# A gated cross-attention layer: VectorE makes both rope products of a block in one instruction, and the maxima of a pair of items in one

## What is computed

```python
q_hk  = (layernorm(x) @ Wq.T).reshape(B, S, H, K)            # 16 heads of 128
q_big = einsum('bshk,hkq->bshq', q_hk, w_kc_q)               # 192 per head
q_big = q_big * cos + rotate_half(q_big) * sin               # rope over halves of 96
q_r   = einsum('bshq,hqr->bhsr', q_big, W_qr)                # 64
k_r   = einsum('bld,hdr->bhlr', rope(ctx), W_kr)
attn  = softmax(einsum('bhsr,bhlr->bhsl', q_r, k_r))         # 256 x 256
ctx_c = einsum('bhsl,bld->bhsd', attn, rope(ctx))
x     = x + tanh(g0) * (ctx_c through w_kc_kv and Wo)
x     = x + tanh(g1) * top-8-of-64 expert biases of layernorm(x)
```

## Time and profile before

| what | before |
|---|---|
| three timed executions | 262.70, 262.97, 262.98, median 262.97 |
| profiled execution | span 261.0 from first to last instruction; its time as a whole is not listed, the timed ones lie 1.7 to 2.0 above this span |
| TensorE matmul busy | 248.7 (95%) |
| VectorE busy | 180.5 (69%), 435 instructions |
| ScalarE busy | 144.0 (55%) |
| GpSimd busy | 136.6 (52%) |

### The profile page before, as it was taken

One profiled execution on the slowest core, in us unless ns is written; L12 is line 12 of the kernel. 1 busy time (PEld: TensorE's weight loads), 2 busy tenths in 40 slices (PEclk: granted clock), 3 DMA queues, 4 the chain that ended last, 5 costly groups with the idle time before them and its releaser, 6 DMA issues.

```text
span 261.0 us, 5668 instructions
## 1 busy us (share of the span) xinstructions
PE 248.7 (95%) x1961; PEld 187.1 (72%) x1961; DVE 180.5 (69%) x435; ACT 144.0 (55%) x440; POOL 136.6 (52%) x221
## 2 busy tenths in 40 slices
PE   6998999999999999999999999999999999889993
PEld 6874777587776878587857876787668758666871
DVE  3799889468775858386847774777658556676575
ACT  2720566574466454746445636656655477758551
POOL 3535139642782278525744565458624952527542
PEclk9999999999999999999999999999999999999997
DMA  6986542534100250124200300030003000000112
GB/s 229 231 224 162 178 102 82 136 106 136 41 0 3 50 173 3 43 58 92 82 3 0 80 4 0 14 70 3 1 0 82 2 3 0 1 3 0 41 34 91
DMA packets 17852, 16.72 MB, mean 64 GB/s; under 512 B 5152, under 2 KB 16544, under 8 KB 17824
## 3 DMA queue, kind: packets, MB, share of 16 engines
q1 hardware_dynamic: 17184, 15.64, 22.7%
q10 hardware_dynamic: 640, 0.72, 0.9%
HBM read 11.11 MB, written 1.05 MB: 47 GB/s over the span
## 4 chain that ended last, share of the span: by engine, by line
PE 79%; DVE 6%; POOL 5%; DMA 4%; ACT 3%; issue 3%; ACTq 0%; DVEq 0%; POOLq 0%
PE ring L1124 23%; PE probs_t L1308 12%; PE scores L1297 9%; PE context L1341 9%; PE ring L1165 5%; PE ring L1090 4%; PE ring L1188 2%; PE ring L1184 2%; PE ring L1186 2%; PE ring L1151 2%; DMA w_kc_q_sb<-in_w_kc_q 2%; POOL roped L599 2%; DMA moved<-cross 2%; PE ring L1113 1%; ACT probs L775 1%
## 5 line engine op out<-in xcount | busy, mean ns | idle before, releaser
L669 POOL TENSOR_SCALAR probs<-probs,inv_sum 128x256 f32<-128x256 f32 x128 | 59.6, 478 | 87.6 <-DVE inv_sum L1028 87.5
L785 ACT COPY probs_t_sb<-probs_t 128x512 f32<-128x512 f32 x64 | 37.6, 588 | 57.7 <-PE probs_t L1308 57.7
L775 ACT ACTIVATE probs<-scores,neg_max 128x256 f32<-128x256 f32 x128 | 59.9, 478 | 4.0 <-DVE neg_max L1022 3.8
L599 POOL TENSOR_TENSOR roped<-roped,cross 128x512 f32<-128x512 f32 x30 | 37.8, 1281 | 11.5 <-DVE cross L866 11.4
L1022 DVE TENSOR_REDUCE neg_max<-scores 128x2 f32<-128x512 f32 x64 | 40.9, 680 | 2.2 <-PE scores L1297 1.9
L1124 PE MATMUL ring<-xn_hi,a_hi 128*128 128x512 f32 x96 | 40.7, 424 | 0.1
L1308 PE MATMUL probs_t<-ident,probs 128*128 128x128 f32 x256 | 40.4, 280 | 0.3 <-POOL probs L669 0.3
L1124 PE MATMUL ring<-xn_hi,a_lo 128*128 128x512 f32 x96 | 37.7, 393 | 0.0
L865 DVE TENSOR_TENSOR roped<-ring,rope_q_sb 128x512 f32<-128x512 f32 x48 | 32.8, 684 | 6.9 <-PE ring L1124 6.7
L1124 PE MATMUL ring<-xn_lo,a_hi 128*128 128x512 f32 x96 | 37.5, 391 | 0.0
L1308 PEld LDWEIGHTS probs_t<-ident,probs 128*128 128x128 f32 x256 | 28.7, 140 | 9.8 <-issue 2.2
(11 more groups left out here) (116 smaller groups left out, 464.3 us busy)
## 6 DMA issues: line engine op xcount, KB each, us to landing
moved<-cross SPq DMA_DIRECT2D x30, 128.0 KB, 2.3
wo_t_sb<-in_wo_t SPq DMA_DIRECT2D x4, 512.0 KB, 4.8
w_qr_sb<-in_w_qr SPq DMA_DIRECT2D x4, 384.0 KB, 4.3
wq_sb<-in_wq SPq DMA_DIRECT2D x3, 512.0 KB, 4.0
w_kc_q_sb<-in_w_kc_q SPq DMA_DIRECT2D x3, 384.0 KB, 4.6
x_sb<-in_x SPq DMA_DIRECT2D x3, 256.0 KB, 5.9
out<-x_sb SPq DMA_DIRECT2D x3, 256.0 KB, 2.2
wq_sb<-in_wq SPq DMA_DIRECT2D x2, 256.0 KB, 4.5
```

The lines of the kernel that those rows point to most:

```text
L599: last = nc.gpsimd.tensor_tensor(roped[:, j, k, :], roped[:, j, k, :], cross[:, k, j, :], ALU.add)
L669: last = nc.gpsimd.tensor_scalar(e, e, inv_sum[:, i % 4, half:half + 1], 1.0, ALU.mult, ALU.mult)
L775: last = nc.scalar.activation(probs[:, i % E_BUFS, half, :], scores[:, i % 2, half, :], ACT.Exp, bias=neg_max[:, i % 4, half:half + 1], ac ...
L785: nc.scalar.copy(probs_t_sb[:, i % T_BUFS], probs_t[:]).then_inc(probs_t_ready, 1)
```

## The change

Rope: one `tensor_tensor` makes both products of a block. Its first input is the bank, read twice through a repeated outer axis; its second input is two neighbouring or spread tables; its output is two slots of one tile. For this `roped` and `cross` become slots of one tile `products`, numbered so that the two slots of a block and the sums that read them can be written as a first, a last and a step; and the tables lose their padding, so that the four tables of a row block lie at equal distances. For j = 1 of k = 1 and 2 the crossed product's slot comes first. Loads of the tables, ScalarE's copy of them, the transfers of the swapped products and the sums read and write the same bytes at the new places.

Maxima: one `tensor_reduce` makes the maxima of both items of a pair, 4 x 256 elements per partition, and raises `max_ready` by two when it ends.

The order of the instructions on every engine stays as it was; on VectorE two that followed each other become one, 48 times for rope and 32 times for the maxima. Nothing else is added or removed on any engine. Core of the diff:

```diff
+SLOT_OF_CROSS = ((10, 11), (0, 8), (1, 9))
...
-        rope_q_sb = sb("rope_q_sb", [P, PC, 2, 2 * S + PAD])
+        rope_q_sb = sb("rope_q_sb", [P, PC, 4, S])
...
-        roped = sb("roped", [P, 2, PC, SPAN])
-        cross = sb("cross", [P, PC, 2, SPAN])
+        products = sb("products", [P, 4 * PC, SPAN])
...
+        def slot_of_roped(k, j):
+            return 2 + PC * j + k
+
+        def roped(k, j):
+            return products[:, slot_of_roped(k, j), :]
+
+        def cross(k, j):
+            return products[:, SLOT_OF_CROSS[k][j], :]
+
+        def spread(first, last):
+
+            return slice(first, last + 1, last - first)
...
-                queue.dma_start(moved[to], cross[at:at + 32, 0]).then_inc(moved_in, 16)
+                queue.dma_start(moved[to], products[at:at + 32, 10:12, :]).then_inc(moved_in, 16)
...
-                q = bank(u).rearrange("p (b s) -> p b s", b=2)
                 to = 1 - j if k else j
-                straight = rope_q_sb[:, k, j:j + 1, 0:S].broadcast_to([P, 2, S])
-                crossed = rope_q_sb[:, k, to:to + 1, S:2 * S].broadcast_to([P, 2, S])
-                nc.vector.tensor_tensor(roped[:, j, k, :].rearrange("p (b s) -> p b s", b=2), q, straight, ALU.mult)
-                last = nc.vector.tensor_tensor(cross[:, k, to, :].rearrange("p (b s) -> p b s", b=2), q, crossed,
-                                               ALU.mult)
+                if k and j:
+                    slots, tables = spread(SLOT_OF_CROSS[k][to], slot_of_roped(k, j)), slice(1, 3)
+                else:
+                    slots = spread(slot_of_roped(k, j), SLOT_OF_CROSS[k][to])
+                    tables = slice(0, 4, 3) if k else slice(2 * j, 2 * j + 2)
+                last = nc.vector.tensor_tensor(
+                    products[:, slots, :].rearrange("p t (b s) -> p t b s", b=2),
+                    bank(u).rearrange("p (o b s) -> p o b s", o=1, b=2).broadcast_to([P, 2, 2, S]),
+                    rope_q_sb[:, k, tables, :].rearrange("p t (o s) -> p t o s", o=1).broadcast_to([P, 2, 2, S]),
+                    ALU.mult)
                 last.then_inc(ring_free, 1)
...
-                dve.wait_ge(scores_ready, i + 1)
-                nc.vector.tensor_reduce(neg_max[:, i % 4, :], scores[:, i % 2], AX_X, ALU.max,
-                                        negate=True).then_inc(max_ready, 1)
+                dve.wait_ge(scores_ready, i + 2)
+                nc.vector.tensor_reduce(neg_max[:, i % 4:i % 4 + 2, :], scores[:], AX_X, ALU.max,
+                                        negate=True).then_inc(max_ready, 2)
...
-            for i in range(LEAD):
-                maxima(i)
+            maxima(0)
...
                     if i % 2 == 0 and i + LEAD < items:
                         maxima(i + LEAD)
-                        maxima(i + LEAD + 1)
```

More of the change, by code:

```diff
@@ L475, in load_rope @@
                     table = rope_q[64:128, 0, (0, 3, 2, 1)[2 * half + t]].rearrange("(j p) s -> p j s", j=2)
-                    queue.dma_start(rope_q_sb[32 * half:32 * half + 32, 0, :, S * t:S * (t + 1)], table
+                    queue.dma_start(rope_q_sb[32 * half:32 * half + 32, 0, t:t + 3:2, :], table
                                     ).then_inc(rope_q_in[k], 16)
                 return
-            queue.dma_start(rope_q_sb[0:64, k, :, 0:2 * S],
-                            rope_q[0:64, k - 1].rearrange("p (i t) s -> p i (t s)", i=2)).then_inc(rope_q_in[k], 16)
+            queue.dma_start(rope_q_sb[0:64, k], rope_q[0:64, k - 1]).then_inc(rope_q_in[k], 16)
         def swap_quarters(queue, quarters=range(4)):
@@ L598, in rope_sums @@
                 for j in range(2):
-                    last = nc.gpsimd.tensor_tensor(roped[:, j, k, :], roped[:, j, k, :], cross[:, k, j, :], ALU.add)
+                    last = nc.gpsimd.tensor_tensor(roped(k, j), roped(k, j), cross(k, j), ALU.add)
                 last.then_inc(rope_ready, 1)
@@ L605, in add_moved @@
                 for j in range(2 if n else 1):
-                    last = nc.gpsimd.tensor_tensor(roped[:, j, 0, :], roped[:, j, 0, :], moved[:, j, :], ALU.add)
+                    last = nc.gpsimd.tensor_tensor(roped(0, j), roped(0, j), moved[:, j, :], ALU.add)
                 last.then_inc(moved_sums, 1)
@@ L698, in pieces @@
                         act.wait_ge(rope_q_in[k], 16 if k else 64)
-                        nc.scalar.copy(rope_q_sb[64:128, k, :, 0:2 * S], rope_q_sb[0:64, k, :, 0:2 * S]
-                                       ).then_inc(rope_q_ready, 1)
+                        nc.scalar.copy(rope_q_sb[64:128, k], rope_q_sb[0:64, k]).then_inc(rope_q_ready, 1)
                     elif kind == "logit":
@@ L874, in first_sums @@
                 dve.wait_ge(moved_in, 64)
-                nc.vector.tensor_tensor(roped[:, 1, 0, :], roped[:, 1, 0, :], moved[:, 1, :], ALU.add
-                                        ).then_inc(shared_sum, 1)
+                nc.vector.tensor_tensor(roped(0, 1), roped(0, 1), moved[:, 1, :], ALU.add).then_inc(shared_sum, 1)
                 dve.wait_ge(ring_free, freed[u])
-                nc.vector.tensor_tensor(roped[:, :, PC - 1, :], roped[:, :, PC - 1, :], cross[:, PC - 1], ALU.add
+                k = PC - 1
+                both = products[:, spread(slot_of_roped(k, 0), slot_of_roped(k, 1)), :]
+                nc.vector.tensor_tensor(both, both, products[:, spread(*SLOT_OF_CROSS[k]), :], ALU.add
                                         ).then_inc(shared_sum, 1)
@@ L1150, in start_rank_queries @@
                     to = slice(64 * j, 64 * j + 64)
-                    nc.tensor.matmul(bank(u)[to, :], m[0:64, unit(0, j), :], roped[0:64, j, 0, :],
+                    nc.tensor.matmul(bank(u)[to, :], m[0:64, unit(0, j), :], roped(0, j)[0:64],
                                      start=True, stop=False, skip_group_check=True)
-                    nc.tensor.matmul(bank(u + 1)[to, :], m[64:128, unit(0, j), :], roped[64:128, j, 0, :],
+                    nc.tensor.matmul(bank(u + 1)[to, :], m[64:128, unit(0, j), :], roped(0, j)[64:128],
                                      start=True, stop=False, skip_group_check=True)
@@ L1164, in rank_queries @@
                         to = slice(64 * (k - 1), 64 * k)
-                        first = nc.tensor.matmul(bank(u - 1)[to, :], m[0:64, unit(k, j), :], roped[0:64, j, k, :],
+                        first = nc.tensor.matmul(bank(u - 1)[to, :], m[0:64, unit(k, j), :], roped(k, j)[0:64],
                                                  start=False, stop=(j == 1), skip_group_check=True)
-                        second = nc.tensor.matmul(bank(u)[to, :], m[64:128, unit(k, j), :], roped[64:128, j, k, :],
+                        second = nc.tensor.matmul(bank(u)[to, :], m[64:128, unit(k, j), :], roped(k, j)[64:128],
                                                   start=False, stop=(j == 1), skip_group_check=True)
```

## The result

The changed kernel takes 265.37 us (median of four executions, 265.28 to 265.47) where the kernel before takes 262.98 beside it (262.70 to 263.21). The ratio is 1.0079, with a 95% interval from 1.0056 to 1.0103: **slower by 0.8%**, 2.4 us. The forecast was 264.2 us, range 262.7 to 265.4. The profiled execution has a span of 263.5 us for 261.0.

The account below looks back on a forecast made before the run. The prediction took TensorE, almost never idle from about 32 to 220 us, as the bound. Stalls from late first maxima less two small gains summed to +1.25 us on 262.97, giving 264.2 us, range 262.7 to 265.4.

Parts of the forecast that it names:

- first rival: Half or all of the stalls are hidden by room before the scores: about 263.1 us; chance 0.18.
- fourth rival: Fused rope products take 2.28 us each, delaying blocks at the start and before 200 us: +5, 268 us; chance 0.02.
- Part 1: Second pair, 35 to 43 us: late exponential delays TensorE's scores by 0.33 us and its turn by 0.28 more.
- Part 2: Pairs at 177 and 183 us: first exponentials start 0.64 and 0.54 us late, costing +0.2 us for both.
- Part 6: At 210.74 us TensorE waits for GpSimd, whose sums began with a rope block at 200 us: -0.06 us.
- Part 3: Pair at 216 us: the whole 0.54 us delay reaches the next scores, less about 0.1 of room: +0.45 us.
- Part 4: Last pair: some 0.18 us of delay passes through ScalarE's context copy to the product at 241.10 us: +0.15 us.
- Part 5: Start: the transfer of swapped products begins after two faster products of block 0, gaining nothing to 0.12: -0.1 us.
- Mostly this is absorbed: In most pairs the 0.54 us delay costs nothing: ScalarE idles over 0.5 us before its copy, or scores are needed later.
- Hidden: Scores have more room, so half or all of the stalls go: 262.8 to 263.4 us, about 263.1; chance 0.18.
- faster: VectorE's shorter queue shows at the start and the rope block at 200 us: 262.3 us; chance 0.08.
- More pairs pay: Four or five more pairs, with little idle time before the copy, each pay about 0.3 us: 265.6 us; chance 0.06.

Follow-up runs that it names:

- E11: Fused rope with separate maxima, the later loads held back until the swapped products have landed; 263.26 us, ratio 0.9990 to the kernel before.
- E7: The changed kernel with ScalarE making one weight split (`a_hi`) ahead of the late exponential; 265.31 us, ratio 1.0071 to the kernel before.
- E3: The changed kernel with maxima fused in six chosen pairs alone, separate in the other 26; 265.32 us, ratio 1.0074 to the kernel before.
- E4: The changed kernel with maxima separate in those six pairs, fused in the other 26; 263.85 us, ratio 1.0014 to the kernel before.
- E8: The changed kernel run again with nothing altered; 265.62 us, ratio 1.0076 to the kernel before.

## Why the prediction was right, and where it fell short

The sign and its cause were right: VectorE's shorter queue is worth nothing, and the late first maximum costs. The sum was +1.25 us; measured are 2.4 in time and 2.3 on TensorE's instructions.

That the time lies in the range is luck. It lies 0.03 us below the upper end of 265.4, and nothing in the prediction gives that end: its bounds of the sum reach +2.1, which is 265.1. The bounds don't follow from their own rule either. Five stalls that are 0.2 us larger add 1.0, so +2.25 (and half of the stalls is 0.7, not the 0.6 of the first rival). The measured 2.4 lies beyond both. One of the prediction's own signs of being wrong came, too: TensorE has new stalls at 59, 78, 105 and 188 us, where it listed none.

- **Prices.** 1.23 and 1.22 us forecast, 1.218 and 1.216 measured. A block of two products took 1.29 us, the fused one 1.22; the saving of 0.06 holds, not the 0.14 that the prediction worked out from the Trainium skill ("VectorE: DVE Perf Modes", "The DRAIN you can't avoid"). It took one sentence of that section for the whole: the section goes on that a next instruction that is not held starts earlier, and the rows agree, with 0.61 us from start to start and a length of 0.69. The fused products that run beside GpSimd's sums take no longer (1.20 us at 40.98, while L618 runs at 40.10), and L894, with two inputs in SBUF, again 2.29 beside a sum of 1.77 (two such sums take 2.54 at 40.10). That agrees with the Trainium skill, "SBUF — State Buffer", "Who interferes with whom", and disposes of the fourth rival.
- **Part 1** (second pair): exponential forecast at 36.96, measured 36.93; scores 39.95 and 39.94; +0.33 and +0.28 came as +0.32 and +0.30.
- **Part 2** (177 and 183 us): 0.2 forecast, 0.19 measured. **Part 6**: -0.06 and -0.09. **Part 3** (216 us): 0.45 and 0.52; there was less room than the 0.1 us assumed. The prediction read the start of the scores from the chain's row, at 218.51, 0.24 us behind ScalarE. The scores' first instruction starts at 218.44, 0.17 behind; in the changed kernel it starts 0.14 behind, so the room was 0.03.
- **Part 4** (last pair): 0.15 forecast. Between 219.5 and 245 us TensorE lost 0.36. Of that, 0.23 arises at 241 us, at the products of the last contexts, as described; 0.13 in the pairs before.
- **Part 5** (start): -0.1 forecast, 0 measured. The last transfer was issued 0.2 us earlier (15.99 for 16.19) and landed when it had (20.93 for 20.94); E11 points at the loads beside it. The step that failed is "From nothing to 0.12: **-0.1**", as far as single traces with a spread of 0.3 us can say.
- **What was missing: "Mostly this is absorbed".** The reason given for this looks at ScalarE's idle time before its next copy and at the scores, and leaves out the other pieces that stand in ScalarE's order. At 59 us it is a split of weights, on which VectorE and TensorE hang in turn: +0.35 (E7). At 188 us it is a rope block on VectorE, behind the reciprocal that waits for the late exponential, a path that the prediction named but did not follow here. The reciprocal starts 1.67 us later than before, GpSimd's sums of that block end at 189.37 for 187.77, and the product that needs them starts 1.44 later, where TensorE was 1.32 late so far; with the product behind it the step is +0.17. E3, which fuses this pair, has the step (0.17) and E4, which doesn't, has none; no run tried it alone. At the ranks' products at 78 and 105 us there are steps of 0.05 and 0.07, which E4 has too and E3 not; with some drift they make the 0.16 between 62 and 150 us. Together 0.7 of the 1.0 us by which the sum was short; the rest is parts 3 to 5.
- **The rivals.** "Hidden" and "faster" are excluded by the interval. "More pairs pay" had nearly the right time (265.6), but the wrong way: it had pairs pay 0.3 us each through the copy. E4 shows that the pairs outside the six pay 0.3 all together. One pair, the one at 56 us, pays through `a_hi`.

The lines at 188 us, of the kernel before and then of the changed one:

```profile
183.82 0.17 DVE L1028 RECIPROCAL inv_sum<-row_sum 128x2 f32<-128x2 f32 x1 [0.49 <-ACT probs L775]
...
185.26 2.51 POOL L599 TENSOR_TENSOR roped<-roped,cross 128x512 f32<-128x512 f32 x2 [0.24 <-DVE cross L866]
...
188.08 0.59 PE L1165 MATMUL ring<-roped,m_sb 64*64 64x512 f32 x1
```

```profile
185.49 0.17 DVE L1044 RECIPROCAL inv_sum<-row_sum 128x2 f32<-128x2 f32 x1 [1.09 <-ACT probs L786]
...
186.86 2.51 POOL L611 TENSOR_TENSOR products<-products 128x512 f32<-128x512 f32 x2 [0.18 <-DVE products L878]
...
189.52 0.61 PE L1179 MATMUL ring<-products,m_sb 64*64 64x512 f32 x1
```

## What to carry to other kernels

Two instructions on an engine that is not the bound are not the same as one of their joint length: if another engine waits for the first result, joining them hands that result over later by nearly the second one's length (0.54 us here), and everything queued behind the waiting engine moves with it. Before fusing, list for the first result who waits, and walk through *all* that stands behind that waiter in program order until the engine that bounds the kernel asks for something. The total of a wait tells little: 13.6 us of it in 26 pairs cost 0.3 us, 3.2 us in 5 places cost 1.9.

## What the runs showed of the hardware

The end of the program ran at a granted clock that differed between two executions of one kernel. TensorE idles in parts there (busy 0.27 to 0.91 of each us from 254 to 260 us, in both). In the first execution of the changed kernel its clock stayed at 1.00 (2.4 GHz) until its work was over, and in E8, the same kernel, it fell to 0.50 (1.2 GHz) at 258 us (stretch; length; busy us of PE, PEld, DVE, ACT, POOL; granted clock; DMA). First the changed kernel, then E8:

```profile
258.00:259.00 1.00, 0.65 (x3) 0.41 (x3) 0.88 (x7) 0.21 (x1) 0.17 (x1) 1.00 0.00 0
259.00:260.00 1.00, 0.40 (x3) 0.27 (x2) 0.96 (x6) 0.26 (x1) 0.38 (x1) 1.00 0.02 8
```

```profile
258.00:259.00 1.00, 0.77 (x2) 0.55 (x3) 0.88 (x6) 0.09 (x1) 0.29 (x1) 0.69 0.00 0
259.00:260.00 1.00, 0.56 (x3) 0.09 (x1) 0.96 (x6) 0.26 (x1) 0.26 (x1) 0.50 0.02 8
```

E8's TensorE is 0.1 us ahead of the first execution at 256 us and ends 0.70 us behind it (261.14 for 260.44). That alone is 0.3% of the time, as much as the smaller effects here, and one reason why steps were read from instructions well ahead of the end.
